# Per-engine places for five feed-forward steps inside the attention loop, and another order of two second layers

## What is computed

```python
def reference(x, ctx, ...):
    # attention: 16 heads of 8, K and V from ctx, Q from layernorm(x)
    k, q, v = split(ctx @ Wk.T + bk), split(ln(x) @ Wq.T + bq), split(ctx @ Wv.T + bv)
    score = einsum('bhij,bhkj->bhik', k, q) / sqrt(8)
    attn = softmax(score, axis=1)                  # over the heads
    x = x + (attn-weighted v) @ Wo.T + bo
    # feed-forward: three residual blocks of two 128x128 linear layers
    h = ln(x)
    for blk in range(3):
        y = layernorm(linear(h, 2 * blk)) * gamma + beta
        h = linear(gelu(y), 2 * blk + 1) + h       # linear: dequantised weight plus a rank-32 product, plus bias
    return x + h
```

## Time and profile before

| | us |
|---|---|
| three runs | 384.17, 386.40, 386.48 |
| median of the runs | 386.4 |
| the profiled execution, its own time | 385.28 |
| its span, first to last instruction | 383.5 |
| outside the span | 1.78 |
| granted TensorE clock, mean | 0.986 |
| PE busy | 342.6 (89%) |
| DVE busy | 327.6 (85%) |
| ACT busy | 289.3 (75%) |
| POOL busy | 267.3 (70%) |

### The profile page before, as it was taken

The page is one execution under the profiler, slowest core; times in us unless marked ns, Lnnn a source line. Parts: engine busy times, 40 slices in busy tenths (PEclk is TensorE's granted clock), DMA queues, the critical chain, the costliest instruction groups (busy, mean ns, idle before and its releaser), DMA issues.

```text
span 383.5 us, 12988 instructions
## 1 busy us (share of the span) xinstructions
PE 342.6 (89%) x4772; PEld 251.7 (66%) x4772; DVE 327.6 (85%) x826; ACT 289.3 (75%) x577; POOL 267.3 (70%) x264
## 2 busy tenths in 40 slices
PE   3766899999999999999979777878999999999975
PEld 2343566677667766776656555765888788887854
DVE  6338999999999999999999989668888989978751
ACT  7746887888788878888767436558889989899862
POOL 6322898788877987888797969658777877773311
PEclk9989999999999999999999998999999999999997
DMA  5593775576547754775543200000000010001011
GB/s 162 151 277 107 238 208 163 153 235 196 173 141 228 205 171 150 213 209 180 163 139 112 84 2 2 1 2 2 28 30 28 27 55 27 30 28 56 27 57 55
DMA packets 53122, 43.29 MB, mean 113 GB/s; under 512 B 4496, under 2 KB 46944, under 8 KB 53088
## 3 DMA queue, kind: packets, MB, share of 16 engines
q1 hardware_dynamic: 53088, 42.84, 37.2%
HBM read 26.05 MB, written 16.78 MB: 112 GB/s over the span
## 4 chain that ended last, share of the span: by engine, by line
PE 55%; DVE 26%; issue 9%; POOL 3%; ACT 3%; DMA 2%; POOLq 0%; DVEq 0%; SPq 0%; ACTq 0%
PE score_ps L1231 8%; PE att_ps L1207 6%; DVE zsum L691 6%; DVE negmax L677 6%; PE score_ps L1157 5%; PE wo_ps L1029 5%; DVE st L714 4%; PE score_ps L1041 3%; PE work L1065 3%; PE work L1289 3%; PE work L1071 2%; PE score_ps L1225 2%; PE work L1078 2%; DMA x_all<-in_x 2%; PE score_ps L1297 2%
## 5 line engine op out<-in xcount | busy, mean ns | idle before, releaser
L441 POOL TENSOR_TENSOR probs<-probs,rz 128x1024 f32<-128x1024 f32 x64 | 136.2, 2138 | 38.6 <-DVE rz L694 38.3
L452 POOL TENSOR_TENSOR rs<-ve,minus_half 128x4 f32<-128x4 f32 (+1 forms) x50 | 59.3, 1186 | 49.1 <-DVE ve L630 36.0
L880 ACT ACTIVATE probs<-score_ps 128x1024 f32<-128x1024 f32 x64 | 65.6, 1026 | 21.8 <-PE score_ps L1157 21.4
L677 DVE TENSOR_REDUCE negmax<-score_ps 128x64 bf16<-128x1024 f32 x64 | 75.1, 1174 | 4.1 <-PE score_ps L1041 4.1
L691 DVE TENSOR_REDUCE zsum<-probs 128x64 f32<-128x1024 f32 x64 | 77.3, 1207 | 0.8 <-ACT probs L880 0.8
L1231 PEld LDWEIGHTS score_ps<-lin_t,h 128*128 128x128 f32 x320 | 38.3, 191 | 17.8 <-DVE h L753 16.4
L928 ACT ACTIVATE z<-score_ps,rs 128x128 f32<-128x128 f32 x160 | 45.9, 383 | 2.0 <-POOL rs L452 2.0
L1231 PE MATMUL score_ps<-lin_t,h 128*128 128x128 f32 x320 | 42.9, 281 | 4.7 <-DVE h L753 2.6
L1157 PE MATMUL score_ps<-negmax,ident_bf 128*128 128x512 bf16 x128 | 39.2, 388 | 8.4 <-DVE negmax L677 8.3
L1029 PEld LDWEIGHTS wo_ps<-wo_t,att_t 128*128 128x128 f32 x256 | 37.5, 193 | 13.8 <-issue 12.2
L1207 PE MATMUL att_ps<-probs,v_diag 128*32 128x64 f32 x2048 | 43.9, 225 | 2.3 <-POOL probs L441 2.1
(11 more groups left out here) (184 smaller groups left out, 671.0 us busy)
## 6 DMA issues: line engine op xcount, KB each, us to landing
q_parts<-parts SPq DMA_DIRECT2D x16, 512.0 KB, 3.5
k_stack<-k_parts SPq DMA_DIRECT2D x32, 256.0 KB, 3.3
q_stack<-q_parts SPq DMA_DIRECT2D x64, 128.0 KB, 2.9
ctx_sb<-in_ctx SPq DMA_DIRECT2D x16, 256.0 KB, 3.7
k_parts<-parts SPq DMA_DIRECT2D x16, 256.0 KB, 2.9
out<-x_all SPq DMA_DIRECT2D x16, 256.0 KB, 2.3
x_all<-in_x SPq DMA_DIRECT2D x14, 256.0 KB, 3.8
x_all<-in_x SPq DMA_DIRECT2D x1, 512.0 KB, 5.0
```

Of the source, the lines that this page charges most:

```text
L441: nc.gpsimd.tensor_tensor(e[:, :, :, :], e[:, :, :, :], by_query.broadcast_to([P, BANDS, SEQ, ADJ]), ALU.mult).then_inc(s_probs, 1)
L452: nc.gpsimd.tensor_tensor(rs2[v][:, lo:hi], ve2[v][:, lo:hi], minus_half[:, lo:hi], ALU.pow).then_inc(p_rs[v], 1)
L677: nc.vector.tensor_reduce(negmax[p % 2][:, :], score_ps[p % 2][:, :].rearrange("p (h k) -> p k h", k=SEQ), AX_X, ALU.max, negate=True).the ...
L880: nc.scalar.activation(probs[p][:, :, :, :], score_ps[p % 2][:, :].rearrange("p (u s k) -> p u k s", s=ADJ, k=SEQ), ACT.Exp, scale=SCALE). ...
```

## The change

The table of places is now one per engine, with a place of its own for steps 2 to 4 (step 3 on PE is not in the table but written into the chunk). PE does tiles 1 to 3 of chunk 14's output product together at (16,0). In a step, PE and DVE handle block 2 first, then block 3, then block 1, where they handled block 3 first.

```diff
-EARLY = {0: (12, 3), 1: (13, 3), 2: (15, 0), 3: (16, 0), 4: (16, 2)}
+EARLY = {"PE": {0: (12, 3), 1: (13, 3), 2: (15, 0), 4: (16, 2)},
+         "DVE": {0: (12, 3), 1: (13, 3), 2: (15, 1), 3: (16, 0), 4: (16, 3)},
+         "ACT": {0: (12, 3), 1: (13, 3), 2: (15, 2), 3: (15, 3), 4: (16, 2)},
+         "POOL": {0: (12, 3), 1: (13, 3), 2: (15, 1), 3: (16, 0), 4: (16, 2)}}
 FIRST_STEP = 5
...
-        def early_steps(c, p, step):
+        def early_steps(eng, c, p, step):
 
             if isinstance(c, int):
-                for t, place in EARLY.items():
+                for t, place in EARLY[eng].items():
                     if place == (c, p):
                         step(t, t % 2)
...
@@ DVE, step
-                if live(t - 7):
-                    k = t - 7
-                    dve.wait_ge(p_c[3], k + 1)
-                    nc.vector.tensor_tensor(x_all[:, k, :, :], by_token(bank[6]), x_all[:, k, :, :],
-                                            ALU.add).then_inc(p_out, 1)
-                for v, k in ((2, t - 5), (1, t - 3)):
-                    if live(k):
+                for v, k in ((2, t - 5), (3, t - 7), (1, t - 3)):
+                    if v == 3 and live(k):
+                        dve.wait_ge(p_c[3], k + 1)
+                        nc.vector.tensor_tensor(x_all[:, k, :, :], by_token(bank[6]), x_all[:, k, :, :],
+                                                ALU.add).then_inc(p_out, 1)
+                    elif live(k):
...
@@ PE, chunk
+                    if isinstance(c, int) and c == NCHUNK - 1 and p == 3:
+                        step(3, 1)
                     if p == 3 and live(c - 1):
                         pe.wait_ge(s_att_t, c)
                         if some(c - 1):
                             pe.wait_ge(s_x2, c - 1)
                         bias_rows(wo_ps[:, :], 1)
                         project_out(0, att_t[1 - par])
-                    if p < 3 and live(c - 2):
+                    if isinstance(c, int) and c == NCHUNK:
+                        if p == 0:
+                            for t in range(1, TPC):
+                                ins = project_out(t, att_t[par])
+                            ins.then_inc(s_wo, 1)
+                    elif p < 3 and live(c - 2):
                         ins = project_out(p + 1, att_t[par])
                         if p == 2:
                             ins.then_inc(s_wo, 1)
...
@@ PE, step
-                    pe.wait_ge(p_g[3], k + 1)
-                    for i in range(TPC):
-                        ins = nc.tensor.matmul(bank[6][:, TILE * i:TILE * (i + 1)], g[2][:, TILE * i:TILE * (i + 1)],
-                                               lin_t[:, 5, :], start=False, stop=True, skip_group_check=True)
-                    ins.then_inc(p_c[3], 1)
-                for v, k in ((2, t - 5), (1, t - 3)):
+                for v, k in ((2, t - 5), (3, t - 7), (1, t - 3)):
                     if live(k):
                         pe.wait_ge(p_g[v], k + 1)
-                        if some(k):
-                            pe.wait_ge(p_h[v], k)
-                        nc.tensor.matmul(second_layer_bank(v, t), lin_t[:, 2 * v - 1, :], g[v - 1][:, :], start=True,
-                                         stop=True).then_inc(p_c[v], 1)
+                        if v == 3:
+                            for i in range(TPC):
+                                ins = nc.tensor.matmul(bank[6][:, TILE * i:TILE * (i + 1)],
+                                                       g[2][:, TILE * i:TILE * (i + 1)], lin_t[:, 5, :], start=False,
+                                                       stop=True, skip_group_check=True)
+                            ins.then_inc(p_c[3], 1)
+                        else:
+                            if some(k):
+                                pe.wait_ge(p_h[v], k)
+                            nc.tensor.matmul(second_layer_bank(v, t), lin_t[:, 2 * v - 1, :], g[v - 1][:, :],
+                                             start=True, stop=True).then_inc(p_c[v], 1)
```

More of the change, by code:

```diff
@@ L445, in chunk @@
                         input_variance(c + 3)
-                    early_steps(c, p, step)
+                    early_steps("POOL", c, p, step)
             def norm_scales(v, lo, hi, count):
@@ L702, in chunk @@
                         first_layer_seeds()
-                    early_steps(c, p, step)
+                    early_steps("DVE", c, p, step)
             def input_stats(k):
@@ L888, in chunk @@
                     input_columns(c + 2)
-                early_steps(c, 0, step)
+                early_steps("ACT", c, 0, step)
                 if live(c):
@@ L895, in chunk @@
                     q_low(c + 2, par)
-                early_steps(c, 1, step)
+                early_steps("ACT", c, 1, step)
                 if live(c - 1):
@@ L908, in chunk @@
                     k_low(c + 2, par)
-                early_steps(c, 2, step)
+                early_steps("ACT", c, 2, step)
                 if live(c):
@@ L919, in chunk @@
                     value_blocks(c + 1, 1 - par)
-                early_steps(c, 3, step)
+                early_steps("ACT", c, 3, step)
             def normalise(v, k, lo, count, src):
@@ L1219, in chunk @@
                         k_remainder(c + 2, par)
-                    early_steps(c, p, step)
+                    early_steps("PE", c, p, step)
             def transpose_z(v, k, dst, i=0):
```

## The result

The changed kernel takes 379.41 us (median of four runs, 377.41 to 380.3), the kernel before 385.71 (four runs). The ratio is 0.984, 95% interval 0.980 to 0.988: 6.3 us less, where 6.7 were forecast. Measured again with the experiments it came to 378.15 against 385.57, ratio 0.982 [0.9785, 0.9855].

The account below looks back on a forecast made before the run. DVE was taken as full to about 220 us, no engine from 230 to 260, then PE. Change-over 3.2 plus steps 3.5 make 6.7 off 386.4: 379.7, predicted 379.5; range 378 to 381, 8 in 10 from 376.5 to 383.3.

Parts of the forecast that it names:

- The sum: Whole kernel: 3.2 + 3.5 = 6.7 us less, from a median of 386.4 to 379.7; 379.5 predicted.
- The change-over, minus 3.2: Where attention ends and steps begin: step 5 starts at 251.0 in place of 254.2, 3.2 us earlier.
- Both holds: DVE's combining instructions in steps 2 and 3 wait for POOL multiplications to end; one takes 0.6 to 1.2 us in step 2.
- Rival (a): Change-over: POOL does not hold DVE's combining instructions; gains 4.6 + 3.5, giving 378.3 us; chance 0.12.
- (f): Change-over: granted clock falls in step 3, some 2 us of its matmuls double; 381.5 us; chance 0.08.
- The steps, minus 3.5: Steps 7 to 16: block 2 ahead of block 3 on PE and DVE shortens ten steps by 3.5 us.
- 7.5 for all ten steps: Steps 7 to 16: each lasts 7.5 us in place of 7.85, with PE, DVE and POOL loops at 7.43 to 7.5.
- The steps after 16: Less work for PE there, waits for Gelu or POOL; gain 0.1 us together, or nothing.
- (b): Only the change-over pays; steps stay at 7.85 because POOL, DVE or ACT closes up; 383.2 us; chance 0.12.
- (c): Only the steps pay; PE's earlier step 3 waits for a late exponential, pushing everything back; 382.4 us; chance 0.08.
- (d): Change-over and steps both mostly fail, gain under 2 us; 385 us; chance 0.06.
- (e): Full steps: Gelu of block 2 comes too late for its new place, PE stands; slower, 394 us; chance 0.04.

Follow-up runs that it names:

- the run at full clock: The changed kernel measured once more without any edit: 378.15 us, ratio 0.982 to the kernel before.
- filler: Changed kernel plus 16 additional transposes on PE in its wait for maximum 15.2 and 8 transposing matmuls ahead of step 3: 377.73 us, ratio 0.980.
- the two halves: Changed kernel with the new places but the old order on PE and DVE: 380.79 us; with the old places but the new order: 382.56 us.
- the probe: Changed kernel plus one small DVE reduction of one SBUF input ahead of the first combining instruction of steps 2 and 3: single run, 376.54 us.

## Why the prediction was right

**The sum.** 379.5 was forecast, 379.41 measured. Part of that is luck. The sum started from a median of 386.4 for the kernel before, which with its fourth run became 385.71, and it ended at 379.7, of which 0.2 was taken off without a reason; so a base too high by 0.7 was partly made up for by a gain put too high by 0.4. The 6.7 stands for a change that by the profile is 5.6 in one execution and 7.4 by the medians of the second measurement, and single runs of one kernel spread over 3 us.

**The change-over, minus 3.2.** Right. By its steps, from the addition of chunk 12 (my numbers less 221.13, the first profile's less 222.88): step 2 ends at 9.1, measured 9.1; last sum and reciprocal 17.0, measured 17.0; POOL's last multiplication 19.7, measured 19.6; h of step 3 20.4, measured 20.2; step 5 29.9, measured 30.7, and 29.7 in the run at full clock. Both holds were there at 0.70 and 1.03 (row durations), and the runs showed that they are holds. Rival (a) falls. What failed in the first profile is that I held (f) for a case apart: the clock did fall during step 3, as the rival had it, and cost 1.0, not 2, and by PE's queue behind step 3, not by h of step 3. Ten of twelve profiles without filler show less than full clock somewhere between 228 and 244 us, the kernel before among them, where DVE was busy without a pause from 228 to 239 and hid it.

**Its parts.** I gave the place of the addition no price of its own; it is 1.8. I said that nobody is late by PE's step 3 standing ahead of the products. At full clock that holds; at the lower clock of the first profile PE was the late one. Of its worth I had not named the larger part, that the old place stands behind PE's wait for chunk 13's addition. The run that put it back shows 3.5 in that profile, with that wait and some lower clock in it. ACT's places and the early tiles of chunk 14 were not put back by themselves, so what each is worth stays open.

**The steps, minus 3.5.** The mechanism was right, the size off: 2.8 in ten steps. h starts directly behind the x statistics, PE is at 7.47 in steps 14 to 16 (7.46 worked out) and the opening weight load no longer shows. The mis-sized term is 7.5 for all ten steps, which measured 7.57. By the starts of h of block 2 on DVE, step 7 with its combining row of 0.65 took 7.44, as put on step 6's showing, but step 8 took 8.00, and in the loop they take 7.42 and 7.65 in turn. The long ones are steps 8, 10 and 12, where DVE idles 0.49, 0.24 and 0.24 ahead of its second combining instruction. The trace of the kernel before had that idle too (0.24 ahead of 310.72, in a step of 7.95 where its neighbours took 7.72), and I gave it no term. The steps after 16 gave 0.4 where 0.1 was put.

**The rivals.** (b) and (c) fall with the two halves run apart, and (d) with the measured 6.3. (e), Gelu late for block 2, did not happen: in step 12 it ends at 308.65 + 0.78 = 309.43 and the matmul starts at 309.68, the same slack of 0.25 as foreseen. It did happen in the last steps (19 and 20), where the second layer waited 0.43 and 0.67; steps 17 to 21 were 0.41 shorter than before all the same. A slower kernel was near all the same, by a way I had not listed: the order on PE without the order on DVE.

## What to carry to other kernels

Engines that hand work to each other need not meet at the same place of the program; place each step on each engine by what it waits for there, and look at what a waiting instruction has queued behind it. When two engines share an order, change it on both: here, on top of the new places, PE's alone made the kernel 2% slower than before and DVE's alone gave 0.8 us in ten steps, too little for the medians to show (ratios 0.9885 and 0.989); both together gave 2.8 us in ten steps. Before moving a small VectorE instruction of two SBUF inputs, look at what GpSimd does then.

## What the runs showed that I had not expected

A small instruction added on DVE in steps 2 and 3 made other steps shorter: in the probe's profile steps 8, 10 and 12 last 7.63, 7.52 and 7.51 against 7.99, 7.64 and 7.63 in the changed kernel's second profile, and the idle 0.49 and 0.24 ahead of the second combining instruction of these steps is gone. Nothing in those steps was edited. The same idle is gone in the two kernels with the last multiplication on DVE, the only others that give DVE one instruction more ahead of the steps, and it is there with the filler, which adds to PE alone. In those two step 8 lasts 7.61 and 7.62, but step 10 lasts 7.79 and 7.80. Where DVE's code lies in memory may be the cause; that was not tried.
